# Causal attention in a decoder kernel: where TensorE issues a group's products with the values

## What is computed

```
q = split_heads(x @ Wq.T + bq)
k = split_heads(x @ Wk.T + bk)
v = split_heads(x @ Wv.T + bv)
q_lr = jnp.einsum('bhtd,hdr->bhtr', q, Wq_lsr)
k_lr = jnp.einsum('bhtd,hdr->bhtr', k, Wk_lsr)
scores = jnp.einsum('bhir,bhjr->bhij', q_lr, k_lr) * scale
scores = jnp.where(causal_mask, jnp.float32(-jnp.inf), scores)
attn = jax.nn.softmax(scores, axis=-1)
y = jnp.einsum('bhij,bhjd->bhid', attn, v)
y = y.transpose(0, 2, 1, 3).reshape(Bq, Tq, D_MODEL)
return y @ Wo.T + bo
```

## Time and profile before

| | |
|---|---|
| median of 3 runs | 2763.75 us (2757.05 to 2773.28) |
| the profiled execution's own time | 2759.56 us |
| its span | 2757.8 us |
| the stage's unit loop, first scores to last `attend` | 2038.0 to 2360.3 us of the span |
| TensorE busy over the span | 2457.9 us (89%) |
| VectorE, ScalarE, GpSimd busy | 64%, 49%, 42% |
| mean granted TensorE clock | 0.961 of full speed |

### The profile page before, as it was taken

How to read it: one execution, slowest core, us unless ns; L and a number is a source line. 1 busy time by engine, 2 the same in 40 slices (tenths; PEclk the granted TensorE clock), 3 DMA queues, 4 the chain that set the end, 5 groups by cost and what they waited for, 6 DMA issues and landing times. The chain is left out here.

```text
span 2757.8 us, 47258 instructions
## 1 busy us (share of the span) xinstructions
PE 2457.9 (89%) x18594; PEld 1493.3 (54%) x18594; DVE 1752.8 (64%) x3198; ACT 1356.7 (49%) x2386; POOL 1149.9 (42%) x612
## 2 busy tenths in 40 slices
PE   5989999999997769999998799999979888788899
PEld 2334434344343324454545588999945555577657
DVE  2799989998999847787777541111236666466433
ACT  4566565666655336667675431111246666232331
POOL 2789889988889813434343201222220000200030
PEclk8999999999999989999999999999989999899999
DMA  5031230311304063444344235555320000200030
GB/s 220 1 130 38 86 138 1 122 70 69 123 9 160 0 178 68 93 88 96 71 83 114 49 126 189 180 186 178 105 74 1 1 1 1 92 9 1 1 109 31
DMA packets 126108, 227.21 MB, mean 82 GB/s; under 512 B 7904, under 2 KB 97504, under 8 KB 109760
## 3 DMA queue, kind: packets, MB, share of 16 engines
q1 hardware_dynamic: 122144, 213.95, 24.8%
q0 software_dynamic: 3744, 10.23, 1.0%
HBM read 201.74 MB, written 22.41 MB: 81 GB/s over the span
## 5 line engine op out<-in xcount | busy, mean ns | idle before, releaser
L208 POOL TENSOR_TENSOR m_h<-m_h,m_bc 128x1024 f32<-128x1024 f32 x256 | 612.2, 2411 | 79.1 <-DVE m_h L521 79.1
L521 DVE TENSOR_TENSOR_SCAN m_h<-m_da,m_h 128x1024 f32<-128x1024 f32 x256 | 578.3, 2275 | 42.6 <-ACT m_da L411 42.5
L281 PE MATMUL m_psy<-m_h,m_ident 128*128 128x512 f32 x1024 | 492.8, 613 | 24.3 <-POOL m_h L208 24.3
L411 ACT ACTIVATE m_da<-x_rows,m_a_neg 128x511 f32<-128x511 f32 x512 | 330.7, 680 | 153.6 <-DVE m_h L521 150.3
L942 POOL TENSOR_SCALAR c_pr<-c_pr,c_share 128x512 f32<-128x512 f32 x128 | 200.0, 1563 | 374.6 <-DVE c_share L1224 374.6
L281 PEld LDWEIGHTS m_psy<-m_h,m_ident 128*128 128x128 f32 x1024 | 196.6, 197 | 292.1 <-issue 234.3
L508 DVE TENSOR_TENSOR m_h<-m_dtx,m_bc 128x1024 f32<-128x1024 f32 x192 | 231.7, 1207 | 24.4 <-PE m_psy L281 18.0
L227 PE MATMUL m_rot<-early_ctx,early_w 128*128 128x512 f32 x240 | 134.2, 688 | 60.5 <-ACT m_gz L387 42.1
L1107 ACT ACTIVATE c_pr<-c_pr,c_low 128x512 f32<-128x512 f32 x256 | 180.9, 707 | 3.6 <-DVE c_low L1216 3.5
L988 PE MATMUL c_psS<-c_kT,c_qT 64*128 64x512 f32 x512 | 147.1, 652 | 32.3 <-DVE c_low L1216 28.4
L1113 ACT ACTIVATE c_pr<-c_pr,c_share 128x512 f32<-128x512 f32 x128 | 92.3, 721 | 161.1 <-DVE c_share L1224 160.7
(11 more groups left out here) (396 smaller groups left out, 4019.1 us busy)
## 6 DMA issues: line engine op xcount, KB each, us to landing
m_bc<-bc_dram SPq DMA_DIRECT2D x32, 2048.0 KB, 8.9
e_up<-in_up SPq DMA_DIRECT2D x39, 1024.0 KB, 5.1
c_vr<-v_dram SPq DMA_DIRECT2D x128, 256.0 KB, 5.0
v_dram<-c_stage SPq DMA_DIRECT2D x32, 256.0 KB, 2.3
e_down<-in_down SPq DMA_DIRECT2D x8, 1024.0 KB, 12.6
e_down<-y_dram SPq DMA_DIRECT2D x8, 512.0 KB, 7.5
h_w<-in_w SPq DMA_DIRECT2D x2, 2048.0 KB, 14.8
m_taps<-in_taps SPq DMA_DIRECT2D x1, 2560.0 KB, 12.1
```

The costliest lines, as they stand in the source:

```text
L208: pool.tensor_tensor(hq, hq, bc[:, 1, NP * s:NP * (s + 1), :], ALU.mult).then_inc(p_ready, 1)
L281: mm = pe.matmul(bank, ident[:], h[:, n % HB, e, :], start=False, stop=(s == NG - 1 and e == NP - 1))
L411: ins = act.activation(da[:, n % 2, e, at:at + L - 1], dt[:, u, j, at:at + L - 1], ACT.Exp, scale=a_neg[:, u, j, NP * s + e:NP * s + e + 1])
L521: dve.tensor_tensor_scan(flat, decay, flat, 0.0, ALU.mult, ALU.add).then_inc(scanned, 1)
```

## The change

`attend` no longer stands in the slots o = 1 (blocks 0 and 1) and o = 3 (blocks 2 and 3). All four blocks are issued at o = 2, behind the scores of that slot and ahead of its `turn`. The rest of the branch is rewritten so that it does what it did.

```
                         scores(n + 2)
                         scores(n + 3)
+                    if n >= 8 and o == 2:
+                        for k in range(LT):
+                            attend(n // 8 - 1, k)
                     if n < TOTAL:
                         turn(n)
                     if n >= 8:
                         q = n // 8 - 1
-                        if o < LT:
-                            if o % 2 == 1:
-                                attend(q, o - 1)
-                                attend(q, o)
-                        elif o == 4:
+                        if o == 4:
                             total(q, numbers[n, "total"])
                         elif o == 5:
                             expand(q, numbers[n, "expand"])
                         elif g == 0 and (n, "out%d" % (o - 6)) in numbers:
                             out(o - 6, numbers[n, "out%d" % (o - 6)])
-                        elif g == 0:
+                        elif o >= LT and g == 0:
                             last_half()
```

## The result

The changed kernel takes 2781.3 us (median of 6, 2773.37 to 2785.44) against 2760.17 us (median of 6 in the same comparison, 2757.05 to 2773.28): ratio 1.0068, 95% interval 1.0043 to 1.0093, slower by 0.7%, about 21 us, with an interval of 12 to 26 us. The forecast was 2779 us. The profiled execution took 2779.49 us, its span 2777.7 us against 2757.8.

What follows compares the result with a forecast made beforehand. With projections TensorE alone sets the pace; without, a chain over TensorE and VectorE. 6 x 0.81 + 2 x 1.5 + 7 x 1.14 = 15.9 us on the median 2763.75 gave 2779 us, range 2767 to 2793.

Steps and rivals of the forecast that it cites:

- The block itself: All four `attend` blocks in one piece cost 2.29 us, not 2.42: a gain of 0.13 us a group.
- Groups with projections: Six groups lose 0.81 us each, waiting at projections B and D until bank psX is emptied.
- With statistics: Two projection groups with layer norm statistics on VectorE between A and its emptying lose 1.5 us each.
- Groups without: Seven groups without projections lose 1.14 us each: scores wait for `row_max(3)`, then `row_max(5)` for `turn(2)`.
- its buffer: In groups without projections, `row_max(5)` writes the buffer that `turn(2)` reads, so it waits for `turn(2)`.
- the copy ahead of it: In groups without projections, VectorE copies the result of `turn(2)`, 0.61 us, before `row_max(5)`.
- the group's bound: Last batch's second group, already waiting 2.21 us for `row_max(3)`: loss goes toward 1.7 us.
- The clock falls more often: Rival, 13 in 100: added TensorE idle brings two to four more clock falls, 23 to 30 us slower in all.
- Half hidden: Rival, 12 in 100: VectorE slack leaves the seven groups without projections losing about 0.4 us; sum 11 us or less.
- Faster: Rival, 5 in 100: early scores of 4 and 5 remove the 1.03 us wait before scores 6 and 7; at most 9 us.

Runs made afterwards that it cites:

- the block ahead of B: All four `attend` blocks at o = 1, behind `turn` and ahead of projection B, against the kernel before: loop 330.3 us, ratio 1.0058.

## Why the prediction was right

**The block itself.** 2.30 us from start to next start (2125.26 to 2127.56), against the 2.29 taken from the last group in the earlier trace rows. The gain of 0.12 to 0.13 us a group was there.

**Groups with projections.** Forecast + 0.81: a wait of 0.63 at B and 0.31 at D, less 0.13. Measured from start to start 0.63 and 0.31, less 0.12, and + 0.80 to + 0.89 for the whole group. (The entries in brackets, 0.56 and 0.25, would give only + 0.69, since they leave out the overlap with the row ahead.) With statistics, forecast + 1.5, measured + 1.46; B waited 1.83 us and stood where VectorE let it, as said from the earlier trace rows. The experiment with the block in these groups alone gave 8.0 us, forecast 7.9.

**Groups without.** Forecast waits of about 1.0 and 1.3 us, measured 0.98 and 1.31; forecast + 1.14, measured + 1.20 in the common case. The prediction named two reasons for `row_max(5)` being late, its buffer and the copy ahead of it, and rested the price for all seven groups on the buffer. That reason was not needed: four buffers alone changed nothing, four buffers and the copy moved behind took the wait away.

**The sum.** Forecast 15.9 us, measured 17.3 and 17.0 in the loop of two pairs of profiles. The eight groups with projections came to 7.9 as forecast, within 0.2. The mis-sized term is the seven others at one price. Six of them lost 0.84 to 1.67 us, 7.3 together against 6.8 forecast; the most, 1.67, was lost by the last batch's third, as before the change it had no wait ahead of `turn` at o = 1 to start with. The second of the last batch lost 0.5 to 2.6. There the wait for `row_max(3)` became 3.85 us, with its 384-wide scores 5.15 us behind the 256-wide ones as before. The 512-wide ones followed 7.25 us later where it had been 3.76; the other groups have 5.55. So 1.8 us are the change, near the 1.7 that I had given as the group's bound, and 1.7 are clock: it was at 0.54 behind the wait, and the block took 4.06 us, not 2.36 (in the second profile 3.48).

**The total, and some luck.** 2779 lies closer to 2781.3 than the working deserves. I added 15.9 to a median of three runs that stands 3.6 us above the median of six, and the difference of the medians is 21.1 us, not 15.9; its interval of 12 to 26 us holds both. Some 4 of the 21 us lie outside the loop or in scatter, where I had put nothing. That the slowdown came out above 0.5% was a near thing, as the prediction said: the interval begins at 0.43%.

**The rivals.** *The clock falls more often*: for this change, no. Lost clock in the loop was 5.1 and 6.8 us against 5.1 and 8.5, and over the whole program the granted clock was 0.959 to 0.963 in six executions, inside the 0.957 to 0.966 of the 39 of the kernel before that were timed with the experiments. The falls moved, and one met the block in both profiles, behind the 3.85 us wait. As a danger of reordering it is real: four other orders lost 12 to 15 us in the loop. The Trainium skill, "TensorE: Matmul & The Clock Gate", section "Loop structure matters more than you think", says that a long wait for a DMA between matmuls lets TensorE go cold, which is the lower clock; the prediction left out "long". The 3.85 us, though a wait for VectorE, agrees, with 0.54 behind it. But the longest wait does not tell how much clock a loop loses: the changed kernel, with 3.85 us, lost 5.1, and the block ahead of B, with no wait over 2.17 us in its loop, lost 12.0. *Half hidden*: no, every group without projections paid. *Faster*: no. The early scores of 4 and 5 bought nothing until VectorE's order was changed too, and even then such a group took 15.55 us, against 15.42 before the change.

## What to carry to other kernels

A short matmul block between two users of one PSUM bank (here psX, between projections A and B) is not only work: it is the time in which the bank gets emptied. Before moving it, ask which copy it lay over, and what will stand there instead. When you read what a wait costs, go from start to start and not by the idle entry alone. And where engines work in fixed orders, more buffers don't help an operation that stands behind a waiting one in its own queue: read the idle entry of that queue's head first.

## What the runs showed of the hardware

Falls of the granted clock to the lower level (1.2 GHz) came in stretches of 3 to 10 us even where TensorE worked without long waits: in the changed kernel the clock fell at 2277.5 us, with no wait over 0.78 us since 2261. Their places shifted from profile to profile for two kernels and not at all for a third. Orders that differ only in where 32 matmuls stand lost 5 or 15 us of clock in a loop of 320 to 338 us. How much of that belongs to the order and how much to how the loop starts is open: only one kernel of the bad kind was profiled twice, and both profiles started alike. It was enough to hide or to double differences of 1 us a group, so the groups' own lengths told what whole times could not.

The 32 matmuls of `attend` cost 2.30 us in one piece, 1.64 + 0.78 = 2.42 us in two halves, and 1.05 + 1.43 = 2.48 us as 8 and 24, each from start to next start at the full clock, with other matmuls behind each piece. From the end of `row_max` on VectorE to TensorE's start it took 0.05 us.
